# An output projection half inside the attention halves of a one-core transformer layer, and one more chunk of each half summed by GpSimd

## The reference

```python
q, k, v = (split(lora_linear(x, W, b, Bm, Am)) for each of q, k, v)
scores = einsum('bhqd,bhkd->bhqk', q, k) * SCALE
attn = softmax(scores, axis=-1)
out = einsum('bhqk,bhkd->bhqd', attn, v)
x = layernorm(x + lora_linear(out, Wo, bo, Bo, Ao))
probs = softmax(x @ Wg); eidx = argmax(probs); gate = probs[eidx]
# each token goes to its expert if there is room (capacity 256)
moe = (silu(xd @ W1[e]) * (xd @ W3[e])) @ W2[e] * gate
x = layernorm(x + moe + (silu(x @ sw1) * (x @ sw3)) @ sw2)
```

## Time and profile before

| | us |
|---|---|
| median of three runs | 1122.74 (1121.78 to 1123.65) |
| the profiled execution | 1124.97 |
| its span, first to last instruction | 1123.3 |
| PE busy | 1064.0 (95%) |
| DVE busy | 725.5 (65%) |
| ACT busy | 552.1 (49%) |
| POOL busy | 472.9 (42%) |

### The profile page before, as it was taken

The page is one execution under the profiler, slowest core; times in us unless marked ns, Lnnn a source line. Parts: engine busy times, 40 slices in busy tenths (PEclk is TensorE's granted clock), DMA queues, the critical chain, the costliest instruction groups (busy, mean ns, idle before and its releaser), DMA issues.

```text
span 1123.3 us, 16277 instructions
## 1 busy us (share of the span) xinstructions
PE 1064.0 (95%) x5710; PEld 738.1 (66%) x5710; DVE 725.5 (65%) x1202; ACT 552.1 (49%) x969; POOL 472.9 (42%) x269
## 2 busy tenths in 40 slices
PE   4899999999999999999999969899999999999995
PEld 3777556465564645555443557678899999998884
DVE  3337967878777787877775478453376666664163
ACT  4220465656566565656657422342356655663125
POOL 2100476884848678484867632047000000003500
PEclk9899999999999999999999989899999999999997
DMA  8556341402423142232356243043357677775604
GB/s 271 198 177 188 101 115 39 95 29 63 116 60 93 39 95 65 58 85 57 95 136 194 83 142 113 19 163 85 85 171 237 211 227 230 222 209 119 93 1 150
DMA packets 154533, 138.40 MB, mean 123 GB/s; under 512 B 43537, under 2 KB 119569, under 8 KB 154208
## 3 DMA queue, kind: packets, MB, share of 16 engines
q1 hardware_dynamic: 147808, 121.58, 38.7%
q0 software_dynamic: 6656, 15.93, 5.1%
HBM read 81.56 MB, written 31.47 MB: 101 GB/s over the span
## 4 chain that ended last, share of the span: by engine, by line
PE 80%; DVE 9%; ACT 3%; DMA 3%; issue 2%; SPq 2%; POOL 0%; ACTq 0%; DVEq 0%
PE bank L751 20%; PE bank L897 12%; PE bank L910 11%; PE bank L845 10%; PE bank L1028 10%; PE bank L833 8%; PE bank L922 4%; PE bank L806 3%; DVE mx L1483 2%; PE bank L758 1%; DMA raw<-in_L_ffn_W_dram 1%; DVE xTlo L1420 1%; DMA at_in<-attn_d 1%; ACT rows L1387 1%; PE bank L784 1%
## 5 line engine op out<-in xcount | busy, mean ns | idle before, releaser
L1483 DVE TENSOR_REDUCE mx<-bank 128x1 f32<-128x512 f32 x512 | 323.5, 680 | 99.1 <-PE bank L845 96.9
L1245 ACT ACTIVATE prob<-bank 128x512 f32<-128x512 f32 x512 | 289.6, 597 | 192.9 <-PE bank L897 179.6
L678 POOL TENSOR_TENSOR psum<-psum,prob 128x1024 f32<-128x1024 f32 x122 | 286.9, 2392 | 0.0
L897 PE MATMUL bank<-Qs,Ks 97*128 97x512 f32 x512 | 208.2, 423 | 1.9 <-DMA Qs<-mrow 0.9
L845 PE MATMUL bank<-Ks,Qs 96*128 96x512 f32 x512 | 188.4, 407 | 2.6 <-DVE mx L1483 1.3
L897 PEld LDWEIGHTS bank<-Qs,Ks 97*128 97x128 f32 x512 | 95.4, 188 | 112.6 <-ACT prob L1245 74.0
L678 POOL TENSOR_TENSOR psum<-prob,prob 128x1024 f32<-128x1024 f32 x32 | 75.8, 2388 | 139.0 <-PE bank L922 135.3
L910 PE MATMUL bank<-prob,V 128*32 128x512 f32 x1024 | 132.6, 606 | 0.0
L845 PEld LDWEIGHTS bank<-Ks,Qs 96*128 96x128 f32 x512 | 96.4, 189 | 44.5 <-DVE mx L1483 13.9
L730 POOL DMA_DIRECT2D oe_d<-oe_sb x16 | 8.8, 548 | 231.4 <-ACT oe_sb L1367 230.4
L833 PE MATMUL bank<-xThi,Wsl 128*128 128x512 f32 x256 | 98.0, 398 | 1.2 <-DVE plane_klo L1473 0.8
(11 more groups left out here) (222 smaller groups left out, 2111.9 us busy)
## 6 DMA issues: line engine op xcount, KB each, us to landing
raw<-in_L_ffn_W_dram SPq DMA_DIRECT2D x120, 256.0 KB, 3.6
Ks<-plane_khi SPq DMA_DIRECT2D x64, 128.0 KB, 2.3
Qs<-plane_qhi SPq DMA_DIRECT2D x64, 128.0 KB, 2.3
raw<-in_L_ffn_sw_dram SPq DMA_DIRECT2D x30, 256.0 KB, 3.6
xin<-in_L_attn_x_dram SPq DMA_DIRECT2D x16, 256.0 KB, 5.3
v_d<-v_sb POOLq DMA_DIRECT2D x16, 256.0 KB, 3.3
Wsl<-wt_d SPq DMA_DIRECT2D x16, 256.0 KB, 4.0
Ks<-plane_klo SPq DMA_DIRECT2D x32, 128.0 KB, 2.3
```

Source lines behind the costliest of these rows:

```text
L678: po.tensor_tensor(psum[:, pr], (prob[0] if kc == 1 else psum)[:, pr], prob[kc % RING][:, pr], ALU.add).then_inc(sem("sum_done"), 1)
L897: nc.tensor.matmul(score_at(v, i), Ks[v.b][0:97, hh, kc * P:(kc + 1) * P], Qs[v.b][0:97, hh, v.hf * HALF:(v.hf + 1) * HALF], start=True, s ...
L1245: ACTV(prob[kc % RING][:, hh, :], score_at(v, i), ACT.Exp, scale=SCALE).then_inc(sem("exp_done"), 1)
L1483: ins = RED(mx[(hf + ahead) % 2][:, 4 * hh + qt, part:part + 1], src, AX.X, ALU.max)
```

## The change

**Sums.** `SUMS` goes from 6 to 7 in 13 halves, stays 6 in one, and goes from 5 and 4 to 7 and 6 in the last two. 

**The split where the values are made.** DVE's `n` now writes the normalised values into the PSUM bank `dn`; a new `h` (ACT) writes their hi part into `attn_hi`, a new `z` (DVE) the lo part into `attn_sb`, and only `z` frees `dn` for the next half's `l` (semaphore `at_done`). SP stores both parts, two DMAs for one; a tile is then loaded as hi and lo, and the splits after the attention (L1267, L1548) are gone.

**Eight tiles earlier.** Tiles 0 to 3 are projected in slot 2 of the last group, tiles 4 to 7 in slot 3: `p` and `q` there mean a quarter of a tile on PE, and its residual and statistics on DVE. All eight use one PSUM bank, so a tile waits until DVE has read the one before. GpSimd's additions of the bias stand between its sums.

**The rest after the attention** has the tiles 8 to 15, a new order on PE, DVE, ACT and SP, and the first normalisation on ACT in place of DVE. 

**The orders** of all halves are new, with one for slot 1 of the last group. **The clearing** of `xd_d` is cut in four, in halves 2, 4, 6 and 8. **SBUF** places are moved so that eight tiles' rows fit beside the attention's buffers.

```diff
-SUMS = [6] * (HALVES - 2) + [5, 4]
+ZERO_HALVES = (2, 4, 6, 8)
+SUMS = [7] * (HALVES - 3) + [6, 7, 6]
+RESIDUAL_BEHIND = {-2: {1: [0], 2: [1], 3: [], 4: [2], 5: [3], 6: []},
+                   -1: {1: [4], 2: [5], 3: [6], 4: [7], 5: []}}
-EVEN = ("mmlvl mm pm m pm m mp mo "
+EVEN = ("mmm vle imm m p m p m mopmmp m "
...
     def norm_out(v):
-            TT(attn_sb[hf][:], attn_sb[hf][:], dn, ALU.mult).then_inc(sem("at_done"), 1)
+            TT(dn, attn_sb[hf][:], dn, ALU.mult).then_inc(sem("norm_done"), 1)
+        def split_lo(v):
+            ve.wait_ge(sem("attn_hi"), v.n)
+            TT(attn_sb[1 - v.hf][:].bitcast(FR), dn, f32(attn_hi[:]), ALU.subtract).then_inc(sem("at_done"), 1)
...
+        def split_hi(v):
+            ac.wait_ge(sem("norm_done"), v.n)
+            if v.n >= 2:
+                ac.wait_ge(sem(f"at_st{v.hf}"), 32 * (v.n // 2 + 1))
+            ACTV(attn_hi[:], dn, ACT.Identity).then_inc(sem("attn_hi"), 1)
...
     # PE
+        def project(t, quarters=range(DC)):
+            if 0 in quarters:
+                pe.wait_ge(sem(f"at_ld{t % 4}"), t // 4 * 32 + 32)
+                if t == 0:
+                    pe.wait_ge(sem("wo_ld"), 32)
+                    pe.wait_ge(sem("pj_done"), PROJECTED)
+                elif t < NT // 2:
+                    pe.wait_ge(sem("y_done"), t)
+                elif t >= NT // 2 + 3:
+                    pe.wait_ge(sem("y_done"), t - 2)
+                    elif w == "p" and v.last and v.slot >= 2:
+                        project(4 * (v.slot - 2) + piece // DC, (piece % DC,))
...
-        for i in range(4):
-            project(i)
-            if i >= 2:
-                logits(i - 2)
-            if i:
-                turn_x1(i - 1)
-        turn_x1(3)
+        for t in range(8, 12):
+            project(t)
+        turn_x1(0, 4)
+        for t in (12, 13):
+            project(t)
+        turn_x1(4, 8)
+        logits(0)
+        for t in (14, 15):
+            project(t)
+        logits(1)
+        turn_x1(8, NT)
...
     # SP, after the halves
         sp.wait_ge(sem("den_done"), 4 * NG)
-        load_shared((13, 0), (13, 1), (2, 0), (2, 1))
+        load_shared((13, 0), (13, 1))
+        store(Half(NG - 1, 4, True))
+        load_at(3)
+        load_xr(3)
```

More of the change, by code:

```diff
@@ L131, in half_order @@
 def half_order(slot, last):
-    if last and slot >= 2:
-        text = LAST_ODD if slot == 3 else LAST_EVEN
+    if last and slot:
+        text = (LAST_FIRST, LAST_EVEN, LAST_ODD)[slot - 1]
     else:
@@ L144, in half_uses @@
     odd = slot % 2
-    uses = smax_uses(1, EARLY[odd]) + ([] if last and slot >= 2 else smax_uses(2, 0, EARLY[1 - odd]))
+    if last and slot:
+        uses = smax_uses(1, EARLY[1]) + smax_uses(2, 0, LAST_EARLY) if slot == 1 else smax_uses(1, LAST_EARLY)
+    else:
+        uses = smax_uses(1, EARLY[odd]) + smax_uses(2, 0, EARLY[1 - odd])
     order = []
@@ L330, in emit @@
     wide = Arena(nc, overlay, sum_at)
-    rows = wide("rows", [P, NT, D], F32)
+    rows_b = wide("rows_b", [P, NT // 2, D], F32)
+    w13 = [[wide(f"w13_{c}{s}", [P, 2, DC, P], FR) for s in ("hi", "lo")] for c in range(2)]
     late = Arena(nc, sum_at, nc.sbuf_usable_end)
@@ L356, in f32, with rows @@
         return ap.bitcast(F32)
+    def rows(t):
+        return (rows_a if t < NT // 2 else rows_b)[:, t % (NT // 2)]
     def w_bank(k):
@@ L1248, in half @@
                             take_ov(v)
+                        elif w == "h" and not v.first:
+                            split_hi(v)
                         elif w == "q" and v.proj:
@@ L1279, in _, with x1_hi @@
         ACTV(wgp[0][:, :, 0:E], wg_raw[:], ACT.Identity).then_inc(sem("wgp_hi"), 1)
-        def x1_hi(i):
-            for j in range(4):
-                turned(i, j, x1_bank(4 * i + j), ("x1_t", 0), "x1_hi")
+        def x1_hi(start, stop):
+            for t in range(start, stop):
+                turned(t // 4, t % 4, x1_bank(t), ("x1_t", 0), "x1_hi")
         def take_logits(i):
@@ L1528, in half @@
                         norm_out(v)
+                    elif w == "z" and not v.first:
+                        split_lo(v)
+                    elif w == "q" and v.last and v.slot >= 2:
+                        tile(4 * (v.slot - 2) + done)
+                        done += 1
         def invert(v, start, stop):
@@ L1616, in step @@
                ALU.subtract).then_inc(sem("hid_lo"), 1)
-        link = Chain(ve, sem("ln1_chain"))
-        for i in range(4):
-            tiles(i, link)
-            variances(link, "ln1")
-            if i:
-                x1_rest(i - 1)
-            scales(link, i + 1, "ln1")
-            for j in range(4):
-                t = 4 * i + j
-                TS(rows[:, t], rows[:, t], mv[:, j, 0:1], ln_r[:, j:j + 1], ALU.subtract, ALU.mult).then_inc(sem("x1_rdy"), 1)
-            if i in FIRST_PROJ:
-                conv(13, FIRST_PROJ[i], 0)
-        x1_rest(3)
+        for t in range(8, 12):
+            tile(t)
+        variances(8, 12)
+        x1_rest(0, 4)
+        scales(2, 8, 12)
+        for t in (12, 13):
+            tile(t)
+        x1_rest(4, 8)
+        conv(13, 0, 0)
+        for t in (14, 15):
+            tile(t)
+        variances(12, NT)
+        scales(3, 12, NT)
+        x1_rest(8, 12)
+        conv(13, 1, 0)
+        x1_rest(12, NT)
+        conv(13, 2, 0)
         step(0, 0, 512)
```

331 lines of the change are left out of this document (184 added, 147 removed), and 12 rows, old and new, of tables (EVEN, LAST_EVEN, LAST_ODD, ODD).

## The result

| | before | changed |
|---|---|---|
| median, both measured together | 1122.26 us (1120.36 to 1123.65) | 1112.74 us (1110.96 to 1113.94) |
| span of the profiled execution | 1123.3 | 1110.5 |

The ratio is 0.9925, 95% interval 0.9903 to 0.9947: 9.5 us faster. The forecast was 26.3 us faster, 1096.4, and its range ended at 1112. The sign was right, the size was not.

What follows compares the result with a forecast made beforehand. PE was taken to bound most attention halves and the feed-forward part, with waits behind the attention. Terms -9 - 4 + 20.8 - 36.1 + 2 = -26.3 us gave 1096.4 us; range 1080 to 1112, its own range 1088 to 1104.

Steps and rivals of the forecast that it cites:

- Clearing in four: Four quarter stores at the starts of odd halves in place of one: cost 0; without cover 4 us, four times.
- Sums in halves 1 to 12: Attention halves 1 to 12: one `l` set less on PE each, GpSimd just fitting; -9 us, between 0 and -10.4.
- The split in the halves: Hi and lo split on ACT and DVE inside each half: cost 0, with one microsecond of cover before PE's `l`.
- the rival of `dn` coming free late: Rival: `z` frees `dn` late, PE stands 2.2 us before `l` in 13 halves; 1125 us, chance 0.07.
- Half 13: Half 13, without projection: maxima spread evenly by the new string, 28.4 us instead of 32.4; -4 us.
- Halves 14 and 15: Last two halves with closing sets: GpSimd's additions bound them, 73.6 us; +20.8 us, from +14.3 to +26.
- The stage behind: From attention to feed-forward: less PE work, with waits of 11.7 us, 47.9 against 84.0; -36.1 us, from -47.8 to -24.4.
- Clock: Behind the attention: one pause of about 3.15 us leaves PE's matmuls at 1.2 GHz for a while; +2 us.
- the prediction's own signs of being wrong: In the new profile: `ones` waiting over 1 us for `z`, stage behind over 56 us, or pairs of halves over 65.
- Its own range: Whole kernel: 1088 to 1104 us, said to come from each term halfway to its ends.
- half of the gain eaten: Rival: transfers and GpSimd eat half, last halves +26, stage -29, clock +3, pairs 5, half 13 4; 1114, chance 0.17.

## Why the prediction was wrong

**Clearing in four, "cost 0; without cover 4 us, four times": the step that failed.** It was priced by what stands behind it in the halves where it is not dangerous ("the next thing behind them (the row maxima) is due 15 us later"). That holds for the quarters behind halves 2 and 6. Behind halves 4 and 8 the next thing on SP is the load of projection weights, which the kernel before already had on the edge. The uncovered cost was put at 4 us a quarter, about right; two of the four stood uncovered, and each pause had a stretch at the half clock behind it: 12.1 us where the forecast has 0. With the quarters elsewhere 5.1 of them stay, at the doubled store, which the forecast did not price here either; with the weights first all of it is gone. These 12.1 us are nearly the whole miss between the profiles (-12.8 for -26.3). The other 3.3 us of the miss in the medians come from taking the change on the profiled 1124.97 for the change on the median.

The row that could have told it was in the trace of before. I read only the landing time of the single store, 16.3 us. SP's own timeline shows what it did to the next issue, the small store that clears the gates' buffer:

```profile
575.34 0.66 SPq L510 DMA_DIRECT2D xd_d<-zeros  x1
576.05 13.62 SPq L512 DMA_DIRECT2D gate_d<-zeros  x1
```

The small store is not what takes the time: in the changed kernel it is issued ahead of a quarter, and there in 0.49 us. So 4 MB of clearing held SP for 13 us more, and 1 MB had to hold it for some 3 (an estimate, a quarter of that; measured 4 to 4.7), and whatever is issued behind it with it. It was harmless there only because nothing was due.

```profile
220.76 0.49 SPq L547 DMA_DIRECT2D gate_d<-zeros  x1
221.30 1.00 SPq L549 DMA_DIRECT2D xd_d<-zeros  x1
```

**Sums in halves 1 to 12, -9: right in size, by a lucky path.** Measured -9.7 with halves 0 and 1 taken in, and with 0.65 us that the kernel before lost around its own short wait in half 4. A pair gained 1.24 us, not 1.74: the new order loses half a microsecond that the count of sets doesn't show. The working took the sets as the cause. The experiments showed that the set alone is worth nothing and needs the order that spreads the scores. GpSimd had its margin: PE's list has no wait for `psum` in these halves, and GpSimd is idle 4.5 us ahead of its first addition in an even half, not 3.

**The split in the halves, 0: right.** PE has no wait for `z` in the halves 1 to 13; the rival of `dn` coming free late did not happen. `z` took 0.68 us each of its 16 times (0.69 at most), with GpSimd adding most of the time, so it was never held for one of GpSimd's additions.

**Half 13, -4: right** (-4.35).

**Halves 14 and 15, +20.8: the mechanism right, the size 2.5 short.** GpSimd bounds them and PE waits for `psum` in both, 3.27 and 1.65 us. GpSimd's additions of half 14 began 9.2 us into the half, not 7.4, and PE ran at the half clock after the first wait (0.96 in the mean of half 15); the forecast's clock term counted only the pause behind the attention.

**The stage behind, -36.1: right** (-34.4). Tile 8's addition held by the router's rest, the wait ahead of the projection of tile 11 (3.7 forecast, 2.3 measured), and ScalarE making x1 before it splits (4.26 us before tile 11 is turned) are in the trace as described. But of these waits only ScalarE's was worth removing.

**Clock, +2**: the stage had 0.89, not 0.95, and the two pauses in the halves had slow stretches of their own, which no term held. Of the prediction's own signs of being wrong one came true: two pairs took over 65 us.

**Its own range.** "Each term halfway to its ends" does not give 1088 to 1104: the terms' ends as stated, all taken halfway at once, give about 1085 to 1111.

The rival that came nearest in time, half of the gain eaten, 1114, named other places: sums of 5 instead of 9, a stage of 55 us, last halves +26. The sums and the stage did not come about, and the last halves, +23.3, lie midway between it and the forecast. The number fits by luck, the mechanism does not.

## What to carry to other kernels

When a transfer is moved to a place in a queue, read the queue at each of its places, not at a typical one: which issue stands behind it there, when the engine that needs it starts, and how long the issuing engine was held behind such a transfer where it stood before. Put loads that the bounding engine waits for ahead of stores that nobody waits for; it took a few lines here and was worth more than the whole change had brought. An instruction taken off the bounding engine gains only if the order lets its neighbours move up: test it with the order and without.

## What the runs showed of the hardware

**A held queue.** The issue of a DMA on SP takes 0.4 to 0.7 us in most of the rows above. Behind 1 MB of clearing two issues of 256 KB loads took 5.38 to 6.07 us, and behind 4 MB a small one 13.62: the store's own issue is short, and the engine pays at the next one. Why it is held there was not tried. The quarter is cut small: the DMA packets under 512 B in 24 us around the first pause are 4708 with it and 604 in the kernel with the quarters elsewhere, 4104 packets for 1 MB, 256 B each. The Trainium skill, DMA: Bandwidth & Descriptors, Specifications, states that below 512 B a transfer does not run at line rate; no run here changed the size of the pieces, so whether larger ones would have held SP for less stays open.

**The slower chips.** The same kernel took 1122.3 us in the first comparison and 1139.4 to 1140.4 on the three chips of the experiments; in the profiles the difference is in the feed-forward part, none in the attention.

**The spread behind the attention.** I had not expected it either (49.4 to 53.5 us for one order of instructions, with a mean clock of 0.89 or 0.90 in the short ones and 0.87 in the two long ones). The traces show one source of it. GpSimd's four bias additions of tiles 12 to 15 start when their `x` has landed, and in the two long profiles that is in the midst of DVE's small instructions for the scales, of 128x4 elements. In the one of 53.1 us:

```profile
663.81 5.03 POOL L731 TENSOR_TENSOR xr<-xr,bo_bc 128x512 f32<-128x512 f32 x4 [10.95 <-DMA xr<-in_L_attn_x_dram]
663.65 0.16 DVE L1649 TENSOR_TENSOR ln_t<-ln_r 128x4 f32<-128x4 f32 x1
663.85 1.27 DVE L1650 TENSOR_TENSOR ln_t<-ln_t,ln_v 128x4 f32<-128x4 f32 x1
665.15 1.22 DVE L1651 TENSOR_SCALAR ln_t<-ln_t 128x4 f32<-128x4 f32 x1
```

Four of them take 1.2 us each there, the length of one bias addition, where they take 0.16 otherwise; in the profile of 53.5 us it is three, in the six short ones two or none. PE's wait for the split of tile 7 grows with them, 3.53 and 2.50 us where the short ones with DVE's old order have 1.1 to 1.4. No run moved these instructions apart, so that this makes up the whole difference is not shown.
